# Row maxima turned by one matmul and subtracted by four row groups, projections in one run, and a new order on all engines

## The chip, the cores and the metric

The kernel runs on one core of one Trainium2 chip. The metric is the device time of one execution in microseconds, the median of several. A core has TensorE (matrix products, PE in the rows; PEld is its loading of the stationary operand), VectorE (DVE), ScalarE (ACT), GpSimd (POOL) and SyncE (SP), each with its own in-order queue, tied together by semaphores. Matrix products are written to PSUM, here one tensor `ps` of eight banks of 512 fp32 columns.

## The reference

One transformer block with modulated layer norms, for 8 batches of 256 tokens of width 128. Attention has 16 heads of 8 and a band mask; the feed-forward part is a mixture of 8 experts of width 64, of which two are chosen per token.

```python
h = _layernorm(x) * (1 + ca) + sa
# attention: B=8, S=256, 16 heads of 8
scores = einsum('bhqd,bhkd->bhqk', Q, K) / sqrt(8)
scores = where(abs(q - k) <= 32, scores, -inf)
out = einsum('bhqk,bhkd->bhqd', softmax(scores), V)
x = x + ga * (out @ W_o.T)
h = _layernorm(x) * (1 + cb) + sb
# experts: 2 groups of 4, then 2 experts of 8, by sigmoid(h @ gate_weight.T) + bias
y = sum_e combine_w[:, e] * ((silu(h @ gate[e].T) * (h @ up[e].T)) @ down[e].T)
x = x + gb * y
```

## The kernel before

One pass of the program handles the eight batches as a software pipeline. While batch i has its attention scores, batch i+1 has its first norm and projections, batch i-1 the end of attention, batches i-2 and i-3 the experts. For each engine the order is written out by hand: `first_step`, `second_step`, `third_step`, then `step(i)` for i = 3, 4, 5, then `seventh_step`, `last_step` and `drain`. Each is a list of calls such as `scores(i, 0)`; each call waits on its semaphores and issues its instructions. Nothing else sets the order, so what stands behind a waiting call on its engine waits too.

Attention of a batch. Queries and keys lie in blocks of 32; a tile `t` (0 or 1) is four query blocks. The 16 heads are four groups (`hg`) of four heads (`g`). `scores(i, t)` (lines 763 and 770) multiplies each key block, spread out by head in `k_bd`, with its two or three neighbouring query blocks of `q_sb`, and adds the mask. Each `hg` uses 32 rows of the array and writes its own PSUM bank 0 to 3: the partitions are (head, key), the columns three cells of 4 x 32 queries. `block_max` (1160) transposes blocks of 32 x 32 and takes each block's maximum, `row_maximum` (1169) the maximum over the three cells; its result lies by (head, query) on the partitions, with 16 numbers for `hg` and query block. The maximum must come off the scores along the columns. For that `shift_rows` (1177), once for each pair of `hg`, writes diagonal blocks of minus the maximum, and `subtract_max` (778) adds them to the scores by a product with a matrix of ones within each head, `quad_ones`: four products of 128 x 128 by 384 columns a tile. `exponentials` (533, ScalarE) makes `probs`, `weigh_values` (797) multiplies them with the values, again by pair: (t, pair) are four parts, which add up in bank OB = 4. `keep_o` (540) copies them to `o_t`; `transpose_o` (876), `normalise_o` (1280, 1284), `transpose_on` (883), `keep_on` (525), `output_projection` (890) and `residual` (1292) give `x1`.

Projections. `project_k` (735), `project_q` (740) and `project_v` (745) stand apart in the order and write banks W2 = 7, W0 = 5 and OB. `keep_k` (1152), `keep_q` (483), `keep_v` (491) copy them. The values go to HBM and back to be laid out by head (`place_values`, SyncE).

Experts. `transpose_x1` (718), `modulate_h2`, `logits` (808, the router), `route_compare`, `route_beats` and `route_weights` (small VectorE instructions), `up` (839 to 841, three fp32r products for each half), `tanh_gate` (546), `gate` (1255) and `gated` (1262), `weigh_experts` (359, GpSimd), `transpose_act` (856), `keep_act_t` (557), `down` (863), `gate_output` (1303), `add_output` (377). They use banks 5, 6 and 7. `keep_clock` (921) issues products whose result is not used, at places where TensorE would pause.

## Time and profile before

| | us |
|---|---|
| median of the timed runs | 164.77 |
| lowest and highest of three | 163.94, 164.79 |
| the profiled execution | 163.83 |
| its span, first to last instruction | 162.0 |
| TensorE busy | 151.1 |
| VectorE busy | 127.1 |
| ScalarE busy | 90.2 |
| GpSimd busy | 55.9 |

The granted clock of TensorE is 1.000 of full speed over the span. Busy time counts overlapping records of an engine once. Records of consecutive matmuls overlap, since their ends are modelled; what a block of matmuls takes from the queue is read from its start to the start of the next. An fp32 product in the program stands as two records; fp32r and bf16 products and fp32 transposes as one.

### The profile page before, as it was taken

The numbers are of one execution on the slowest core, as the hardware profiler recorded it, in microseconds if no ns is written. First come the engines' busy times: TensorE is split into PE (matmuls) and PEld (weight loads), VectorE is DVE, ScalarE is ACT, GpSimd is POOL, SyncE is SP. The second block draws the span as 40 slices with busy tenths as digits, with TensorE's granted clock in tenths as the row PEclk, the third lists the DMA queues.
The fourth block names the chain that finished last, engine by engine and source line by source line (L and its number), as shares of the span: only waits on it lengthen the run. The fifth ranks groups of instructions, "written<-read, shape, count | busy, mean of one in ns | idle before, by whom it ended". The sixth has DMA issues, their size and how long they took to land.

```text
span 162.0 us, 5111 instructions
## 1 busy us (share of the span) xinstructions
PE 151.1 (93%) x1976; PEld 123.2 (76%) x1976; DVE 127.1 (78%) x353; ACT 90.2 (56%) x172; POOL 55.9 (34%) x109
## 2 busy tenths in 40 slices
PE   6799989999899999999999999999999999888993
PEld 2376778787677898978887888789888986674773
DVE  3439496495988999897999789877988898587872
ACT  3234387556666656575747764785166428624740
POOL 6420072021540606521662147212251306426340
PEclk9999999999999999999999999999999999999999
DMA  4874134034103503510351013401250000010002
GB/s 134 239 210 28 8 38 32 4 65 28 10 0 46 59 0 67 37 34 4 65 33 35 0 35 43 32 0 35 34 36 0 9 28 0 6 32 0 0 4 65
DMA packets 47431, 6.23 MB, mean 38 GB/s; under 512 B 42416, under 2 KB 47024, under 8 KB 47408
## 3 DMA queue, kind: packets, MB, share of 16 engines
q1 hardware_dynamic: 47264, 5.90, 23.4%
q8 instruction: 16, 0.26, 0.7%
q14 instruction: 7, 0.06, 0.1%
q10 hardware_dynamic: 144, 0.00, 0.0%
HBM read 3.81 MB, written 2.10 MB: 36 GB/s over the span
## 4 chain that ended last, share of the span: by engine, by line
PE 71%; issue 9%; ACT 8%; DVE 6%; POOL 4%; POOLq 0%; ACTq 0%; DVEq 0%
PE ps L763 11%; PE ps L797 11%; PE ps L863 10%; PE ps L778 5%; PE ps L856 5%; PE ps L921 3%; PE ps L839 3%; ACT probs L533 3%; PE ps L841 3%; PE ps L840 3%; PE ps L718 3%; PE ps L808 2%; PE ps L740 2%; PE ps L745 2%; PE ps L890 2%
## 5 line engine op out<-in xcount | busy, mean ns | idle before, releaser
L1160 DVE TRANSPOSE_TENSOR_REDUCE blkmax<-ps 128x44 f32<-128x1408 f32 x16 | 26.4, 1648 | 11.7 <-PE ps L770 9.5
L797 PEld LDWEIGHTS ps<-probs,v_bd 128*36 128x36 f32 x640 | 21.5, 113 | 7.4 <-issue 4.7
L533 ACT ACTIVATE probs<-ps 128x704 f32<-128x704 f32 x32 | 23.0, 755 | 6.1 <-PE ps L778 5.6
L797 PE MATMUL ps<-probs,v_bd 128*36 128x96 f32 (+2 forms) x640 | 25.1, 228 | 0.8 <-ACT probs L533 0.5
L359 POOL TENSOR_TENSOR act_w<-act,cw 128x512 f32<-128x512 f32 x15 | 15.7, 1044 | 21.7 <-issue 13.7
L763 PEld LDWEIGHTS ps<-q_sb,k_bd 32*128 32x128 f32 x640 | 19.3, 186 | 4.3 <-issue 2.4
L763 PE MATMUL ps<-q_sb,k_bd 32*128 32x96 f32 (+2 forms) x640 | 21.3, 274 | 0.7 <-ACT probs L533 0.5
L778 PE MATMUL ps<-shift,quad_ones 128*128 128x384 f32 x64 | 16.9, 370 | 0.0
L863 PE MATMUL ps<-wd_sb,act_t 128*128 128x128 f32 x128 | 16.2, 280 | 0.6
L863 PEld LDWEIGHTS ps<-wd_sb,act_t 128*128 128x128 f32 x128 | 15.0, 191 | 2.0 <-ACT act_t L557 1.8
L546 ACT ACTIVATE tanh_g<-ps 128x512 f32<-128x512 f32 x14 | 8.3, 596 | 14.4 <-PE ps L841 14.4
L839 PE MATMUL ps<-w_hi,h_hi 128*128 128x512 f32 x32 | 13.4, 419 | 0.7 <-POOL h_lo L371 0.7
L334 POOL TENSOR_SCALAR veps<-mv 128x2 f32<-128x2 f32 x16 | 4.7, 294 | 26.9 <-DVE mv L1135 26.4
L371 POOL TENSOR_TENSOR h_lo<-h_t,h_hi 128x256 fp32r<-128x256 f32 x8 | 5.9, 732 | 22.0 <-ACT h_hi L505 21.9
L1177 DVE TENSOR_TENSOR shift<-row_max,con 128x256 fp32r<-128x256 f32 x32 | 12.8, 432 | 0.5
L841 PE MATMUL ps<-w_hi,h_lo 128*128 128x512 f32 x32 | 12.6, 393 | 0.0
L840 PE MATMUL ps<-w_lo,h_hi 128*128 128x512 f32 x32 | 12.5, 392 | 0.0
L557 ACT ACTIVATE act_t<-ps 128x512 f32<-128x512 f32 x16 | 9.4, 596 | 5.2 <-PE ps L856 5.0
L339 POOL TENSOR_TENSOR rstd<-veps,minus_half 128x2 f32<-128x2 f32 x16 | 11.4, 711 | 1.3
L778 PEld LDWEIGHTS ps<-shift,quad_ones 128*128 128x128 f32 x64 | 10.3, 190 | 1.0 <-DVE shift L1177 0.5
L921 PE MATMUL ps<-idle_bf 128*128 128x512 bf16 x28 | 9.5, 457 | 1.4 <-DVE idle_bf L1500 1.4
L1255 DVE SCALAR_TENSOR_TENSOR gate_a<-tanh_g,ps 128x512 f32<-128x512 f32 x14 | 9.6, 682 | 1.7 <-ACT tanh_g L546 1.4
(108 smaller groups left out, 283.5 us busy)
## 6 DMA issues: line engine op xcount, KB each, us to landing
x_sb<-x SPq DMA_DIRECT2D x8, 128.0 KB, 3.2
v_spill<-v_sb SPq DMA_DIRECT2D x8, 128.0 KB, 2.3
v_bd<-v_spill SPq DMA_DIRECT2D x32, 32.0 KB, 3.1
out<-out_sb SPq DMA_DIRECT2D x7, 128.0 KB, 2.0
wgu_sb<-w_gu SPq DMA_DIRECT2D x1, 512.0 KB, 4.3
wm_sb<-wmod SPq DMA_DIRECT2D x1, 256.0 KB, 3.8
wd_sb<-w_down SPq DMA_DIRECT2D x1, 256.0 KB, 5.2
con<-consts SPq DMA_DIRECT2D x1, 244.0 KB, 3.2
```

The source lines that it names most:

```text
L359: nc.gpsimd.tensor_tensor(act_w[:, t, :].rearrange("p (e i) -> p e i", e=E), act[:, t, :].rearrange("p (e i) -> p e i", e=E), view(cw[:, t ...
L533: nc.scalar.activation(probs[:, t, hgs, cols], ps[:, hgs, cols], ACT.Exp, scale=float(DH) ** -0.5).then_inc(probs_ready, 1)
L763: nc.tensor.matmul(view(ps[:, hg, at:at + 1], [[(QBT - 1) * KB, hi - lo + 1], [1, KB]]), k_bd[rows, kb].rearrange("p g k -> p (g k)"), vie ...
L778: last = nc.tensor.matmul(ps[:, hg, 0:CELLS * KB], quad_ones[:], view(shift[:, hg, 0:1], [[0, 3], [1, QBT * KB]]), start=False, stop=True, ...
L797: last = nc.tensor.matmul(ps[p0:p0 + VW, OB, c0 + lo * KB:c0 + (hi + 1) * KB], v_bd[:, i % VB, kb, hg, :], view(probs[:, t, hg, at:at + 1] ...
L839: nc.tensor.matmul(ps[:, bank, :], h2_hi[:, tok], w_hi[:, w], start=True, stop=False)
L840: nc.tensor.matmul(ps[:, bank, :], h2_hi[:, tok], w_lo[:, w], start=False, stop=False)
L841: last = nc.tensor.matmul(ps[:, bank, :], h2_lo[:, tok], w_hi[:, w], start=False, stop=True)
L863: last = nc.tensor.matmul(ps[:, down_bank(b, t), t * D:(t + 1) * D], act_t[:, t, c, :], wd_sb[:, c, :], start=(c == 0), stop=(c == NC_ - 1))
L921: nc.tensor.matmul(ps[:, bank, :], idle_bf[:, 0:128], idle_bf[:], start=True, stop=True)
L1160: nc.vector.tensor_reduce(blkmax[:, t, :, live(t):live(t) + LIVE], view(ps[:, 0, live(t) * KB:live(t) * KB + 1], [[BANK, NHG], [KB, LIVE], ...
L1177: nc.vector.tensor_tensor(shift[:, pair * PAIR:(pair + 1) * PAIR].rearrange("p h (q k) -> p (h q) k", k=KB), view(row_max[:, pair * PAIR, ...
```

## The change

1. The subtraction of the maxima. `spread_max` (VectorE) writes each of the 16 maxima into the column of its own head, zeros elsewhere, 64 numbers a partition. `turn_max` (TensorE) makes `max_by_head` the stationary operand and the matrix `C_REP` the moving one, 32 columns, into the unused columns 384 to 415 of bank 0. The maxima then lie on partitions by (hg, head, query block), with the 32 queries along the columns. `shift_rows`, now once a tile, multiplies them with -1 in the column of their block. `subtract_max` multiplies with `head_ones`, for each `hg` from its own 32 rows.
2. Queries, keys and values are projected in one call. `k_bd` and `q_sb` have two buffers. Queries and values both go to bank OB.
3. `x_sb` has eight buffers, and SyncE issues all loads of x by the start.
4. On TensorE waits that protect PSUM banks stand in the order instead of in the functions; `keep_act_t` and `keep_on` wait for the last readers of what they overwrite.
5. The written order is new on TensorE, VectorE, ScalarE and GpSimd, from the first step to the drain.

On TensorE, in the middle of a regular step. Before (`h_t` by line 808 is the router's input; 735 and 740 are keys and queries, 797 values times probabilities, `act_w` the weighted experts):
```order
L808 MATMUL ps<-gw_sb,h_t 128x8 x2
L778 MATMUL ps<-shift,quad_ones 128x384 x4
L735 MATMUL ps<-h_t,wqkv_sb 128x256
L797 MATMUL ps<-probs,v_bd 36x32 x2
L797 MATMUL ps<-probs,v_bd 36x64 x2
L797 MATMUL ps<-probs,v_bd 36x96 x4
L797 MATMUL ps<-probs,v_bd 36x64 x2
L740 MATMUL ps<-h_t,wqkv_sb 128x256
L797 MATMUL ps<-probs,v_bd 36x32 x2
L797 MATMUL ps<-probs,v_bd 36x64 x2
L797 MATMUL ps<-probs,v_bd 36x96 x4
L797 MATMUL ps<-probs,v_bd 36x64 x2
```
After, the first half of a regular step, from the router (778) on: 743 is the turn, 751 the subtraction, 809 the down projection, 706 and 819 transposes of x and o_t, 729 the scores:
```order
L778 MATMUL ps<-gw_sb,h_t 128x8 x2
L743 MATMUL ps<-con,max_by_head 128x32
L809 MATMUL ps<-wd_sb,act_t 128x128 x4
L751 MATMUL ps<-shift,head_ones 128x384 x4
L809 MATMUL ps<-wd_sb,act_t 128x128 x4
L706 MATMUL ps<-con,xn 128x128 x2
L819 MATMUL ps<-con,o_t 128x100 x4
L729 MATMUL ps<-q_sb,k_bd 128x32 x4
L729 MATMUL ps<-q_sb,k_bd 128x2x32 x4
L729 MATMUL ps<-q_sb,k_bd 128x3x32 x8
```
The subtraction, before followed by the key projection, stands between the halves of the down projection; the turn stands one half of the down projection ahead of it.

On VectorE, second tile of a regular step. Before:
```order
L1160 TENSOR_REDUCE blkmax<-ps 128x4x11
L1169 TENSOR_REDUCE row_max<-blkmax 128x16
L1177 TENSOR_TENSOR shift<-row_max,con 128x256 x2
L1255 SCALAR_TENSOR_TENSOR gate_a<-tanh_g,ps 128x512
L1262 TENSOR_TENSOR act<-gate_a,ps 128x512
L1152 TENSOR_TENSOR k_bd<-ps,con 128x1024
```
After (1147 block maximum, 1139 keys, 1156 row maximum, 1166 spread, 1252 and 1259 the first token half's gate, 1175 the shift):
```order
L1147 TENSOR_REDUCE blkmax<-ps 128x4x11
L1139 TENSOR_TENSOR k_bd<-ps,con 128x1024
L1156 TENSOR_REDUCE row_max<-blkmax 128x16
L1166 TENSOR_TENSOR max_by_head<-row_max,con 128x4x16
L1252 SCALAR_TENSOR_TENSOR gate_a<-tanh_g,ps 128x512
L1175 TENSOR_TENSOR shift<-ps,con 128x128
L1259 TENSOR_TENSOR act<-gate_a,ps 128x512
```
The copy of the keys moved in front of the row maximum, and the first gate stands between the spread and the shift.

The diff, cut to its core:

```diff
-C_NI = C_MASK + 2 * KB
-C_ONES = C_NI + KB
+C_ONES = C_MASK + 2 * KB
...
+C_QB = C_HEAD + G
+C_END = C_QB + QBT
...
-    c[:, C_NI:C_NI + KB] = np.where(r[:, None] == q[None], -1.0, 0.0)
-    c[:, C_ONES:C_ONES + 128] = g[:, None] == g[None]
+    c[:, C_ONES:C_ONES + 128] = (r // QBT)[:, None] == g[None]
...
+    c[:, C_QB:C_QB + QBT] = np.where((r % QBT)[:, None] == np.arange(QBT)[None], -1.0, 0.0)
...
-        q_sb = sb("q_sb", [128, S])
-        k_bd = sb("k_bd", [128, NKB, G, KB])
+        q_sb = sb("q_sb", [128, 2, S])
+        k_bd = sb("k_bd", [128, 2, NKB, G, KB])
...
-        shift = sb("shift", [128, NHG, QBT * KB], F32R)
+        max_by_head = sb("max_by_head", [128, NHG, KB])
+        shift = sb("shift", [128, QBT, KB], F32R)
...
             place_values(0)
+            load_x(4)
             place_values(1)
-            load_x(4)
+            load_x(5)
             place_values(2)
+            load_x(6)
+            load_x(7)
...
-            def project_k(b):
...
+            def project_qkv(b):
                 wait(pe, h_ready, b, 1, 1)
                 nc.tensor.matmul(ps[:, W2, 0:S], wqkv_sb[:, 1], h_t[:], start=True, stop=True).then_inc(k_ps, 1)
+                nc.tensor.matmul(ps[:, OB, 0:S], wqkv_sb[:, 0], h_t[:], start=True, stop=True)
...
+            def turn_max(i, t):
+                wait(pe, spread_ready, i, QT, t + 1)
+                nc.tensor.matmul(ps[:, 0, CELLS * KB:(CELLS + 1) * KB], max_by_head[:].rearrange("p h m -> p (h m)"),
+                                 con[:, C_REP:C_REP + KB], start=False, stop=True, skip_group_check=True)\
+                  .then_inc(turned_ps, 1)
+
             def subtract_max(i, t, pair):
-                wait(pe, shift_ready, i, PARTS, t * NPAIR + pair + 1)
+                wait(pe, shift_ready, i, QT, t + 1)
                 for hg in range(pair * PAIR, (pair + 1) * PAIR):
-                    last = nc.tensor.matmul(ps[:, hg, 0:CELLS * KB], quad_ones[:],
-                                            view(shift[:, hg, 0:1], [[0, 3], [1, QBT * KB]]),
+                    rows = slice(hg * KB, (hg + 1) * KB)
+                    last = nc.tensor.matmul(ps[:, hg, 0:CELLS * KB], head_ones[rows],
+                                            view(shift[rows, 0, 0:1], [[0, 3], [1, QBT * KB]]),
                                             start=False, stop=True, skip_group_check=True)
                 last.then_inc(shifted_ps, 1)
...
-            def shift_rows(i, t, pair):
+            def spread_max(i, t):
                 wait(dve, rowmax_ready, i, QT, t + 1)
+                wait(dve, turned_ps, i, QT, t)
...
+                nc.vector.tensor_tensor(
+                    view(max_by_head[:, 0, 0:1], [[KB, NHG], [QBT, G], [1, QBT]]),
+                    view(row_max[:, 0, 0:1], [[QBT, NHG], [0, G], [1, QBT]]),
+                    view(con[:, C_DEN:C_DEN + 1], [[0, NHG], [1, G], [0, QBT]]), ALU.mult).then_inc(spread_ready, 1)
+
+            def shift_rows(i, t):
+
+                wait(dve, turned_ps, i, QT, t + 1)
                 wait(dve, shifted_ps, i, PARTS, t * NPAIR)
                 nc.vector.tensor_tensor(
-                    shift[:, pair * PAIR:(pair + 1) * PAIR].rearrange("p h (q k) -> p (h q) k", k=KB),
-                    view(row_max[:, pair * PAIR, 0:1], [[1, PAIR * QBT], [0, KB]]),
-                    view(con[:, C_NI:C_NI + 1], [[0, PAIR * QBT], [1, KB]]), ALU.mult).then_inc(shift_ready, 1)
+                    shift[:], view(ps[:, 0, CELLS * KB:CELLS * KB + 1], [[0, QBT], [1, KB]]),
+                    view(con[:, C_QB:C_QB + 1], [[1, QBT], [0, KB]]), ALU.mult).then_inc(shift_ready, 1)
...
             def step(i):
+                wait(pe, probs_ready, i - 1, PARTS, 4)
                 scores(i, 0)
...
+                turn_max(i, 0)
+                wait(pe, actt_ready, i - 3, NT, 2)
+                down(i - 3, 0)
+                subtract_max(i, 0, 0)
+                subtract_max(i, 0, 1)
```

## Rows read from the trace of the kernel before

**Rows 1.** The page's busy line: busy us, share of the span, instructions.
```profile
PE 151.1 (93%) x1976; PEld 123.2 (76%) x1976; DVE 127.1 (78%) x353; ACT 90.2 (56%) x172; POOL 55.9 (34%) x109
```

**Rows 2.** Stretches: length, busy us of each engine, PEclk, DMA share, GB/s.
```profile
37.07:55.26 18.19, 16.93 (x248) 13.50 (x244) 15.18 (x40) 11.57 (x25) 6.74 (x14) 1.00 0.32 28
72.10:88.90 16.80, 16.61 (x239) 14.19 (x238) 14.69 (x42) 10.81 (x22) 6.78 (x13) 1.00 0.25 33
120.53:139.79 19.26, 18.31 (x266) 15.06 (x262) 14.77 (x40) 11.46 (x24) 6.08 (x10) 1.00 0.04 9
139.79:162.00 22.21, 18.20 (x112) 13.96 (x112) 16.08 (x52) 8.22 (x15) 7.74 (x12) 1.00 0.07 20
```

**Rows 3.** TensorE's timeline in one step: start us, length us, instructions.
```profile
81.12 0.29 PE L770 MATMUL ps<-mask_bf,rep_bf 32*128 32x256 bf16 x4
81.34 1.44 PE L797 MATMUL ps<-probs,v_bd 128*36 128x64 f32 x40
82.71 0.44 PE L718 MATMUL ps<-con,xn 128*128 128x128 f32 x2
...
84.38 0.51 PE L808 MATMUL ps<-gw_sb,h_t 128*128 128x8 f32 x4
84.74 0.95 PE L778 MATMUL ps<-shift,quad_ones 128*128 128x384 f32 x4
85.53 0.59 PE L735 MATMUL ps<-h_t,wqkv_sb 128*128 128x256 f32 x2
86.19 0.82 PE L797 MATMUL ps<-probs,v_bd 128*36 128x32 f32 x20
86.94 0.70 PE L740 MATMUL ps<-h_t,wqkv_sb 128*128 128x256 f32 x2
87.57 0.82 PE L797 MATMUL ps<-probs,v_bd 128*36 128x32 f32 x20
...
93.71 0.61 PE L745 MATMUL ps<-wqkv_sb,h_t 128*128 128x128 f32 x4
94.08 0.59 PE L778 MATMUL ps<-shift,quad_ones 128*128 128x384 f32 x2
94.51 0.60 PE L890 MATMUL ps<-wo_g,on_t 128*128 128x128 f32 x4
94.87 0.60 PE L778 MATMUL ps<-shift,quad_ones 128*128 128x384 f32 x2
95.31 0.39 PE L839 MATMUL ps<-w_hi,h_hi 128*128 128x512 f32 x1
```

**Rows 4.** TensorE's timeline, first projections of batch 0.
```profile
8.09 0.67 PE L735 MATMUL ps<-h_t,wqkv_sb 128*128 128x256 f32 x2 [0.63 <-ACT h_t L475]
...
9.48 0.59 PE L921 MATMUL ps<-idle_bf 128*128 128x512 bf16 x2
```

**Rows 5.** VectorE's timeline in the same step.
```profile
79.50 0.35 DVE L1205 TENSOR_REDUCE rank<-ebeat 128x16 f32<-128x224 f32 x1
...
80.82 0.68 DVE L1255 SCALAR_TENSOR_TENSOR gate_a<-tanh_g,ps 128x512 f32<-128x512 f32 x1
...
82.14 1.64 DVE L1160 TRANSPOSE_TENSOR_REDUCE blkmax<-ps 128x44 f32<-128x1408 f32 x1
83.81 0.21 DVE L1169 TENSOR_REDUCE row_max<-blkmax 128x16 f32<-128x48 f32 x1
84.06 0.76 DVE L1177 TENSOR_TENSOR shift<-row_max,con 128x256 fp32r<-128x256 f32 x2
...
86.54 1.22 DVE L1152 TENSOR_TENSOR k_bd<-ps,con 128x1024 f32<-128x1024 f32 x1
```

**Rows 6.** Groups by form, VectorE: busy us, mean ns; idle before.
```profile
L1311 DVE TENSOR_TENSOR y_last<-ps,gate_row 128x128 f32<-128x128 f32 x2 | 0.6, 292 | 2.0 <-PE ps L863 2.0
```

**Rows 7.** Groups by form, ScalarE: copies of o_t, tanh.
```profile
L540 ACT ACTIVATE o_t<-ps 36x512 f32<-36x512 f32 x16 | 9.4, 589 | 0.4
...
L546 ACT ACTIVATE tanh_g<-ps 128x512 f32<-128x512 f32 x14 | 8.3, 596 | 14.4 <-PE ps L841 14.4
```

More of the change, by code:

```diff
@@ L319, in _ @@
             step(B - 2)
-            for b in range(B - 4, B - 1):
+            for b in range(B - 1 - 3, B - 1):
                 sp.wait_ge(out_ready, b + 1)
@@ L1056, in drain @@
                 output_projection(B - 1)
+                wait(pe, yg_ready, B - 3, 1, 1)
                 up(B - 2, 0)
@@ L1279, in normalise_o @@
                 wait(dve, ot_ps, i, 1, 1)
+                wait(dve, ont_ps, i, 1, 0)
                 nc.vector.reciprocal(
```

597 lines of the change are left out of this document (287 added, 310 removed).

## The prediction, made before the result was known

> **What bounds the kernel now.** I read the busy line first: TensorE is busy 93% of the span, VectorE 78%, ScalarE 56%, GpSimd 34% [rows 1]. Shares are averages, so I then read the stretches [rows 2]. Their bounds are the starts of the key-by-query products of a batch (call them S; S0 and S1 are its two tiles of query blocks). In the regular stage one batch passes every 16.80 us, and TensorE is busy 16.61 of it, VectorE 14.69, ScalarE 10.81, GpSimd 6.78. That is a TensorE bound with VectorE close behind. In 120.53 to 139.79 and from there to the end TensorE leaves 0.9 and 4.0 us idle: the drain is a chain through all engines.
>
> Third, I read one step of TensorE's own queue, start to start, because overlapping records hide what a block costs [rows 3]. The subtraction of the row maxima (line 778) stands there twice: four matmuls adjacent, 84.74 to 85.53, 0.79 us; and split in pairs, 94.08 to 94.51 and 94.87 to 95.31, 0.43 + 0.44. That is 1.66 us a batch. Keys, queries and values stand in three places: 85.53 to 86.19 (0.66, of which some 0.2 waits for the exponentials), 86.94 to 87.57 (0.63), 93.71 to 94.08 (0.37): 1.66. Another 0.2 is TensorE's idle time in the step's stretch, 16.80 - 16.61 [rows 2]. So a step holds 16.4 us of work and 0.4 of waits.
>
> **The subtraction.** The new one uses 32 rows of the array for each of the four head groups, where each used all 128. The nearest row of that form is the mask product: four matmuls on four row groups, 256 columns each, and the next block starts 0.22 us after the first of them [rows 3]. Its 256 columns and the 384 of the subtraction stand in the relation of 0.12 to 0.18 us by the present 0.79/4 for 384. That gives a lower bound of 0.22 + 0.07 = 0.29 us for four. The upper bound is the present 0.79, if they queue one behind another. I take 0.36, near the mask row, with 0.07 for the change from 128-row to 32-row form in front. The turn is one matmul in the program, two in the records, as all fp32 here. The router's product (line 808) is the nearest: four records in 0.36 us, 84.38 to 84.74, so 0.18 for two; the upper bound adds the same gap of some 0.12 that the mask product leaves behind it, 0.30. I take 0.22. A tile then costs 0.58, two tiles 1.16 against 1.66: 0.50 us less per batch. The ends are 2 x (0.29 + 0.18) = 0.94 (0.72 less) and 2 x (0.79 + 0.30) = 2.18 (0.52 more).
>
> The skill has a rule in each direction. The Trainium skill (TensorE: Matmul & The Clock Gate, Part 3) says that four K=32 matmuls on separate row groups start a few ns apart and measured 3.07 times the throughput; by it a tile's subtraction would be 0.79/3.07 = 0.26 us, and the kernel's sum would fall by some 1.6 us more. The Trainium skill (TensorEngine Tiling (Array Packing), Key Properties) also says that a change of the tiling mode drains the engine, which speaks against breaking one 128-row queue by short 32-row pieces; the trace bears this out in kind, since the mask product is left only 0.22 us after its start; what it could take is the rival below in which nothing is gained.
>
> **Projection and value products.** In one run the three projections took 8.09 to 9.48, 1.39 us [rows 4]. With an entry of 0.1 that is 1.49 against 1.66, and most of the difference is the wait. The value products (line 797) pay for it: now two of the four parts are one run, 81.34 to 82.71 (1.37), and the others cost 0.75 each, 2.87 in all; apart, four times 0.75 plus entries, 3.1. That is 0.23 more. The transposes of the activations become one run of eight, with one such gap less, some 0.15. Together these edits are worth 0.1 less; bounds -0.3 and +0.4, from the same rows, by whether an entry costs nothing or 0.15 each. TensorE's work for a step: 16.4 - 0.5 - 0.1 = 15.8, which I round up to 15.9 for the one more change of form.
>
> **VectorE.** Each batch loses four shift instructions of 0.76/2 = 0.38 us [rows 5], 1.5 us, and gains two spreads and two shifts. The spread writes 64 numbers a partition from the 16 of row_max; the nearest row is the row maximum, 0.21 [rows 5], the bound above is today's shift, 0.38. I take 0.24 with the gap. The new shift makes 128 per row and reads PSUM as line 1311 does, 0.29 [rows 6], so 0.33 with the gap. 2 x 0.57 = 1.14, about 0.35 less a batch. VectorE's load falls to 14.3 us plus its gaps; it does not bind by its sum.
>
> It can bind by its order. From block maximum to subtraction the queue now goes VectorE, TensorE, VectorE. Today 0.96 us pass from the end of the block maximum (82.14 + 1.64) to the subtraction at 84.74 [rows 3, 5]. The new round is 0.24 (row maximum) + 0.24 (spread) + 0.05 + 0.37 (a turn until its result, from the router's row: 0.51 less two spacings) + 0.05 + 0.33 = 1.3 us, 0.3 longer. Behind a turn that waits stand, in TensorE's in-order queue, a down projection in the first half of a step, and a value product, the output projection and the subtraction in the second. Laid out from S0 at 0, with the blocks above: S0 1.4, value product 2.1, transposes 3.3, router 3.7; block maximum 1.6 to 3.25, spread done 3.75, so the turn at 3.8 waits 0.1. The down projection waits for ScalarE's second act_t copy, 4.4, 0.3 us. Shifts are ready at 4.9 (a layer norm of 0.8 stands in between, beside the turn), the subtraction runs at 5.4. ScalarE has two copies of o_t (0.59 each, [rows 7]) in front of its exponentials, which end at 7.2; TensorE reaches S1 at 7.4. Block maximum of S1 8.9 to 10.6, keep_k (1.22, [rows 5]), row maximum and spread to 12.3; the turn is reached at 12.3, the second subtraction at 13.7, the last up product at 14.1 to 15.5, the value product to 16.2. Then S0 again. Waits of some 0.4 us stay: 15.9 + 0.4 = 16.3 us a step, 0.5 less.
>
> **The three stages.** Regular part, from S0 of batch 3 (55.26) to S0 of batch 7 (120.53): four steps, 4 x 0.5 = 2.0 us. Start, to 55.26: the chain products, maxima, exponentials, products sets it through the first two batches (the turn's 0.3 more a tile is met by 0.43 less for the subtraction that ends it), S0 of batch 2 comes at 36.8 for 37.07 [rows 2]; seven more clock-keeping matmuls stand in waits. In batch 2 the queue is full and gains as a step does: 0.8 us in all. The x loads of batches 4 to 7, now issued between and behind the first value transfers, cost nothing on SyncE's queue, since x is read a batch later; if they delayed the values of batch 1, 0.3. Last step, 120.53 to 139.79: a step's 0.5 and what the earlier start of its S0 leaves (one value product less before it), but its subtraction is split in pairs and so is paid three times: 0.7. The drain, 22.2 us, keeps its code and its chain: 0. Sum 2.0 + 0.8 + 0.7 = 3.5. The profiled execution took 163.83 (span 162.0 and 1.8 around it), so 160.3 by it; it is 0.9 below the median of the runs, 164.77, against which the forecast is 161.3.
>
> **Rivals.**
> - *The full gain.* The 0.4 us of waits a step fall away too, or the subtraction costs 0.29. A step is 15.9: 4 x 0.9, 1.0 and 1.1 at the ends, 5.7 in all, 159.1. For it: every wait in my layout is under 0.3. Against: ScalarE's copies are where they are.
> - *Nothing is gained.* The changes of form (one more run of value products, two subtractions, each way) cost 0.15 more than I price, and waits for act_t and act take the rest; the step stays at 16.7 and the start gains nothing: 164.4. For it: VectorE and TensorE hand to each other twice more a batch.
> - *Slower by VectorE's loop.* The last up product now stands at the end of a step. After it come the end of its last matmul and tanh (0.2 + 0.6, [rows 7]), gate and product (80.82 to 82.14, 1.32, [rows 5]), then the block maximum and spread of the next batch, 1.64 + 0.5, before TensorE may turn: 4.3 us. TensorE has 4.4 us of work for that time (value product, S0, value product, transposes, router). If the routing weights (1.32 us of small instructions ahead of that gate, 79.50 to 80.82) end later than the tanh by more than 0.1 us, all of that excess is added each step. With 0.9 of it a step is 17.1: 4 x 0.3, 0.3 in the last, 0.6 at the start, 2.1 more, 166.9. My layout has the weights end 0.2 after the tanh, so it decides soon. Against: what makes them late is a late output projection, which would itself come later in a slower step.
> - *The row groups do not run at once* for this type. Then subtraction and turn cost up to 0.52 more a batch, some 0.4 a step of the forecast's work too much: 166.5. Against: the mask row.
>
> **Numbers.** Half a per cent, 0.8 us, is about what a measurement can tell from no change. Forecast 0.50 (its own range 159.8 to 163.0), full gain 0.17, nothing 0.16, VectorE's loop 0.12, no concurrency 0.05. Faster by over 0.8 us: 0.50 + 0.17 = 0.67, and 0.01 of the case without gain, 0.68; within 0.16; slower 0.16. The range that should hold eight in ten runs from 158.6 to 165.2: it takes in the full gain, the case without gain and the near end of the losses.
>
> **What would show it.** In the changed profile the four subtractions of a tile should start within 0.05 us of each other and the block after them follow in 0.3 to 0.4; the turn's records should take under 0.25; S0 to S0 should be 16.0 to 16.6 in batches 3 to 6; the end of VectorE's product of the second act tile should lie just before the block maximum; the drain from the transpose of o_t of batch 7 should be unchanged at about 20 us of queue. A step of 16.8 or more, a turn preceded by more than 0.3 of idle TensorE, or a subtraction over 0.6 would show it wrong, and in that order I would look for the cause.

## The result and the profile after

The changed kernel takes 165.15 us (median of 20 runs, 164.68 to 166.34) against 164.7 for the kernel before beside it: ratio 1.0067, 95% interval 1.004 to 1.0093. It is slower by little, where 161.3 and faster was forecast. The profiled execution has a span of 162.5 us at a granted clock of 0.999. First the busy line of its page, which answers to [rows 1]:

```profile
PE 152.3 (94%) x2010; PEld 122.4 (75%) x2015; DVE 122.0 (75%) x354; ACT 88.5 (54%) x172; POOL 54.5 (34%) x109
```

VectorE lost 5 us of work, as meant, and TensorE gained 1. Two stretches that answer to [rows 2]: a regular step; and from S0 of batch 7 to the transpose of o_n of batch 7. The rest, from there to the end of the span, takes 19.12 us. Columns: stretch, length, then the busy time of each engine, granted clock, DMA share, GB/s.

```profile
70.29:87.23 16.94, 16.93 (x246) 14.25 (x242) 14.19 (x42) 10.38 (x22) 6.57 (x14) 1.00 0.23 26
120.36:143.38 23.02, 21.79 (x308) 17.93 (x307) 19.32 (x60) 13.17 (x26) 9.36 (x15) 1.00 0.08 10
```

A step is 16.94 us for 16.80 [rows 2], and TensorE is busy in 16.93 of it. So no wait shows as idle time, and what TensorE does takes longer. (A wait can hide in the busy time, since the ends of the records are modelled; the pair after_noturn and noturn_early below shows how much.) Its queue in that step, with the blocks that answer to [rows 3] (start, modelled length, operands, array rows and columns):

```profile
72.67 1.04 PE L802 MATMUL ps<-con,act_w 128*128 128x128 f32 x8
73.55 0.56 PE L778 MATMUL ps<-gw_sb,h_t 128*128 128x8 f32 x4
74.05 0.41 PE L743 MATMUL ps<-con,max_by_head 128*128 128x32 f32 x2
74.47 1.16 PE L809 MATMUL ps<-wd_sb,act_t 128*128 128x128 f32 x8
75.56 0.44 PE L751 MATMUL ps<-shift,head_ones 32*128 32x384 f32 x4
75.93 1.16 PE L809 MATMUL ps<-wd_sb,act_t 128*128 128x128 f32 x8
76.92 0.38 PE L706 MATMUL ps<-con,xn 128*128 128x128 f32 x2
...
78.97 0.70 PE L714 MATMUL ps<-h_t,wqkv_sb 128*128 128x256 f32 x2
...
80.30 0.47 PE L791 MATMUL ps<-w_hi,h_hi 128*128 128x512 f32 x1
```

```profile
82.88 0.31 PE L743 MATMUL ps<-con,max_by_head 128*128 128x32 f32 x2
83.12 0.81 PE L767 MATMUL ps<-probs,v_bd 128*36 128x64 f32 x20
83.86 0.71 PE L833 MATMUL ps<-wo_g,on_t 128*128 128x128 f32 x4
84.50 0.45 PE L751 MATMUL ps<-shift,head_ones 32*128 32x384 f32 x4
84.88 0.50 PE L791 MATMUL ps<-w_hi,h_hi 128*128 128x512 f32 x1
85.22 0.40 PE L792 MATMUL ps<-w_lo,h_hi 128*128 128x512 f32 x1
```

Read start to start. The subtraction (751) takes 0.37 and 0.38 us, the second turn (743) 0.24, the first 0.42 (a wait is in it, as after_early shows), the projections in one run 80.30 - 78.97 = 1.33. These are the prices of the forecast. But the blocks around them have grown: the down projection has halves of 1.09 and 0.99, 2.08 in all, where it takes 1.79 in the old order without its wait (before_early, below), and the output projection takes 0.64 for 0.36 [rows 3]. In VectorE's queue [rows 5] the spread and the shift are as small as forecast:

```profile
71.84 1.65 DVE L1147 TRANSPOSE_TENSOR_REDUCE blkmax<-ps 128x44 f32<-128x1408 f32 x1 [0.15 <-PE ps L736]
...
73.76 0.23 DVE L1166 TENSOR_TENSOR max_by_head<-row_max,con 128x64 f32<-128x64 f32 x1
...
74.58 0.26 DVE L1175 TENSOR_TENSOR shift<-ps,con 128x128 fp32r<-128x128 f32 x1
```

Two theories follow. *Changes of form*: the array works in three forms here, 128 rows by 128 columns, 32 rows (scores, mask, new subtraction) and 36 columns (value products); each time the form changes the block before ends later and the block behind starts slower, and this eats what the row groups save. From S0 to S0 the order before changes the form 9 times, the new one 14 times. *Order and waits*: the new order brings waits, and the blocks' growth is these.

### The profile page after: what moved, and what is told of

Read it like the earlier page. It is cut to its first block, busy times and chain, and to the rows that moved or that the text cites. A ratio compares the mean times of both kernels' runs of the same rounds, so it can differ in the third digit from the quotient of the medians.

```text
span 162.5 us, 5181 instructions
## 1 busy us (share of the span) xinstructions
PE 152.3 (94%) x2010; PEld 122.4 (75%) x2015; DVE 122.0 (75%) x354; ACT 88.5 (54%) x172; POOL 54.5 (34%) x109
## 4 chain that ended last, share of the span: by engine, by line
PE 73%; DVE 10%; issue 5%; DMA 3%; SPq 3%; ACT 3%; POOL 2%; POOLq 0%; ACTq 0%
PE ps L767 13%; PE ps L729 11%; PE ps L809 8%; PE ps L802 5%; PE ps L791 4%; PE ps L792 3%; PE ps L793 3%; DMA x_sb<-x 3%; PE ps L751 3%; PE ps L743 3%; PE ps L851 3%; PE ps L706 2%; PE ps L714 2%; PE ps L833 2%; PE ps L819 2%
## 5 line engine op out<-in xcount | busy, mean ns | idle before, releaser
L767 PE MATMUL ps<-probs,v_bd 128*36 128x64 f32 (+2 forms) x640 | 26.2, 228 | 0.3
L326 POOL TENSOR_SCALAR veps<-mv 128x2 f32<-128x2 f32 x16 | 3.6, 224 | 48.1 <-DVE mv L1122 47.7
L809 PE MATMUL ps<-wd_sb,act_t 128*128 128x128 f32 x128 | 17.7, 284 | 0.2
L331 POOL TENSOR_TENSOR rstd<-veps,minus_half 128x2 f32<-128x2 f32 x16 | 12.3, 767 | 9.3 <-ACT xn L450 8.0
L791 PE MATMUL ps<-w_hi,h_hi 128*128 128x512 f32 x32 | 14.0, 438 | 0.9 <-DVE y_g L1301 0.5
L859 PE MATMUL ps<-idle_bf 128*128 128x512 bf16 x30 | 10.1, 446 | 1.8 <-DVE idle_bf L1498 1.4
L1139 DVE TENSOR_TENSOR k_bd<-ps,con 128x1024 f32<-128x1024 f32 x8 | 9.7, 1208 | 1.9 <-PE ps L714 1.9
L527 ACT ACTIVATE o_t<-ps 36x512 f32<-36x512 f32 x16 | 9.5, 591 | 1.9 <-PE ps L767 1.5
L545 ACT ACTIVATE act_t<-ps 128x512 f32<-128x512 f32 x16 | 8.9, 596 | 2.5 <-PE ps L802 2.5
L465 ACT ACTIVATE h_t<-ps,mod 128x256 f32<-128x256 f32 x8 | 6.5, 814 | 6.3 <-PE ps L706 6.3
```

What stands on the lines that cost most here:

```text
L331: nc.gpsimd.tensor_tensor(rs[:], veps[:], minus_half[:], ALU.pow).then_inc(rs_done, 1)
L767: last = nc.tensor.matmul(ps[p0:p0 + VW, OB, c0 + lo * KB:c0 + (hi + 1) * KB], v_bd[:, i % VB, kb, hg, :], view(probs[:, t, hg, at:at + 1] ...
L791: nc.tensor.matmul(ps[:, bank, :], h2_hi[:, tok], w_hi[:, w], start=True, stop=False)
L809: last = nc.tensor.matmul(ps[:, down_bank(b, t), t * D:(t + 1) * D], act_t[:, t, c, :], wd_sb[:, c, :], start=(c == 0), stop=(c == NC_ - 1))
L859: nc.tensor.matmul(ps[:, bank, :], idle_bf[:, 0:128], idle_bf[:], start=True, stop=True)
L1139: nc.vector.tensor_tensor(k_bd[:, b % 2], view(ps[:, W2, 0:1], [[1, NKB], [0, G], [NKB, KB]]), view(con[:, C_HEAD:C_HEAD + 1], [[0, NKB], ...
```

## The experiments

Ratios are to the kernel before on the same chip, with 95% intervals.

**probe.** One look at the kernel before with the new subtraction in the old order, and behind its end a tail of products that wait for no other engine: 128-row fp32 blocks of eight records in turn with the new subtraction, with the old one, and with 36-column products, and each of these once in a run of its own kind.

```diff
+                for _ in range(6):
+                    full(4, 6)
+                    rows32(1)
+                full(4, 6)
+                rows32(6)
```

> A probe behind the last output of a kernel of the order before (it carries the new subtraction; only its tail is read, and that tail is extra work whose results are not used). It issues blocks of a plain fp32 product on 128 rows (F), of the subtraction on four times 32 rows (R), of the old subtraction on 128 rows, and of the value product with 36 columns (W), each once as one run and once in turn with F. Theory 'changes of form': every change between F and R or F and W costs TensorE 0.1 to 0.2 us beyond the blocks themselves, so F, R, F, R takes about 0.3 us more per pair than the same blocks sorted, and F with the old subtraction under 0.1 more. Rival 'waits': a change of form costs nothing by itself (under 0.03 us a pair), and what the changed kernel lost are waits for other engines.

```profile
168.44 6.42 PE L934 MATMUL ps<-con 128*128 128x128 f32 x56
174.78 0.45 PE L941 MATMUL ps<-shift,head_ones 32*128 32x384 f32 x4
175.16 1.16 PE L934 MATMUL ps<-con 128*128 128x128 f32 x8
176.25 0.45 PE L941 MATMUL ps<-shift,head_ones 32*128 32x384 f32 x4
...
183.57 1.32 PE L941 MATMUL ps<-shift,head_ones 32*128 32x384 f32 x24
184.83 1.16 PE L934 MATMUL ps<-con 128*128 128x128 f32 x8
...
188.12 1.05 PE L934 MATMUL ps<-con 128*128 128x128 f32 x8
188.93 0.95 PE L947 MATMUL ps<-shift,head_ones 128*128 128x384 f32 x4
...
195.33 4.49 PE L947 MATMUL ps<-shift,head_ones 128*128 128x384 f32 x24
```

In a run of its own kind the new subtraction takes 1.26/6 = 0.21 us for four. In turn with 128-row blocks it takes 0.38, and the block behind 1.09, where eight such records take (174.78 - 168.44) x 8/56 = 0.91 in a run. So the pair costs 1.47 for 0.21 + 0.91 = 1.12: 0.35 for two changes of form, as the first theory had it. The old subtraction, of the form of its neighbours, takes 0.79 in turn and the block behind it 0.81, 1.60 in all, and costs nothing extra (0.72 + 0.91 in runs). So the new subtraction saves 0.13 a pair, from a block whose own time fell by 0.41. The 36-column products show the same: 0.79 and 1.08 in turn (202.51 to 203.30 and 201.43 to 202.51), 1.87 for at most 0.69 + 0.91, so 0.27 for two changes.

**before_newsub.** The old order with the new subtraction and the turn. The first turn stands two blocks ahead of its subtraction, the second one block, so that the turn's round through VectorE has some cover; the two pairs of the first subtraction, apart before, stand side by side.

```diff
                 down(i - 3, 1)
+                turn_max(i, 0)
                 transpose_on(i - 1)
                 project_v(i + 1)
                 subtract_max(i, 0, 0)
-                output_projection(i - 1)
                 subtract_max(i, 0, 1)
+                output_projection(i - 1)
```

> The order before, with only the subtraction changed: spread, turn, one shift a tile, subtraction on four row groups, its two pairs adjacent. Theory 'changes of form': a step of 16.80 us loses 1.66 and gains 2 x 0.38 (subtraction) + 2 x 0.24 (turn) + 0.4 (first and last matmul of the blocks beside four more changes), 16.8; time within 0.5% of before, ratio 1.00. Rival 'the order is what lost': the subtraction is worth the 0.5 us a batch that I forecast, so 4 us less, ratio 0.976.

169.96 us, ratio 1.036 (1.032 to 1.040): slower than either theory. Its step is 17.43 us with TensorE busy 16.98, so 0.45 of it shows as waiting:

```profile
74.84:92.27 17.43, 16.98 (x243) 13.65 (x243) 14.02 (x42) 10.82 (x22) 6.67 (x13) 1.00 0.25 32
...
87.91 0.29 DVE L1209 TENSOR_TENSOR shift<-ps,con 128x128 fp32r<-128x128 f32 x1 [0.50 <-PE ps L779]
```

The second shift waits 0.50 us for the turn, and the up product in front of that turn takes 0.52 us (86.95 to 87.47) for 0.23 without a wait. So in this order the round from VectorE to TensorE and back costs time. TensorE is busy 0.37 longer than before (16.61), but part of this is such hidden waiting, so the run doesn't say how much work the new subtraction adds. It does not show a gain in work, which speaks for the first theory.

**after_oldsub.** The new order with the old subtraction: both shifts and the 128-row products, no turn.

```diff
-                turn_max(i, 0)
...
-                    rows = slice(hg * KB, (hg + 1) * KB)
-                    last = nc.tensor.matmul(ps[:, hg, 0:CELLS * KB], head_ones[rows],
+                    last = nc.tensor.matmul(ps[:, hg, 0:CELLS * KB], head_ones[:],
```

> The changed kernel with the old subtraction (two shifts a tile, 128 rows, no spread and no turn), all else as changed. Theory 'changes of form': the step of 16.94 us loses the turn with its waits (0.66), the 0.75 of the subtraction and 0.38 beside it, and gains 1.58: 16.7; in all 1.6 us less than the changed kernel, ratio to before 0.997. Rival 'the order is what lost, the subtraction gains': 4 us more than the changed kernel, ratio 1.03.

165.66 us, ratio 1.0088 (1.0058 to 1.0118), neither theory. In the new order the two ways of subtracting come out almost alike in the whole time. One wait appears that the turn had stood in:

```profile
70.05:87.10 17.05, 16.69 (x243) 14.58 (x239) 14.83 (x42) 10.39 (x22) 6.57 (x14) 1.00 0.18 23
...
73.30 0.56 PE L770 MATMUL ps<-gw_sb,h_t 128*128 128x8 f32 x4
74.22 1.16 PE L801 MATMUL ps<-wd_sb,act_t 128*128 128x128 f32 x8 [0.36 <-ACT act_t L544]
```

**after_fullrows.** The new kernel, turn and order kept, but the subtraction on all 128 rows.

```diff
-                    rows = slice(hg * KB, (hg + 1) * KB)
-                    last = nc.tensor.matmul(ps[:, hg, 0:CELLS * KB], head_ones[rows],
-                                            view(shift[rows, 0, 0:1], [[0, 3], [1, QBT * KB]]),
+                    last = nc.tensor.matmul(ps[:, hg, 0:CELLS * KB], head_ones[:, hg],
+                                            view(shift[:, 0, 0:1], [[0, 3], [1, QBT * KB]]),
```

> The changed kernel with one edit: the four subtractions of a tile use all 128 rows of the array again (the stationary operand is zero outside the head group's rows), the turn and the order stay. Theory (the saving of the row groups is mostly eaten by two changes of form per tile): the subtraction's own block grows from 0.37 to 0.79 us, its neighbours shrink by some 0.3 per tile, so a regular step goes from 16.94 to about 17.2 and the whole from 165.15 to about 167, ratio to before 1.014. Rival (the changes of form cost nothing here, neighbours stay): 0.42 us more per tile, 17.8 a step, about 171.5 in all, ratio 1.04.

167.63 us, ratio 1.0237 (1.0202 to 1.0273), a step of 17.17: near the first theory, far from the second's 171.5. The same blocks as above, with nothing else changed:

```profile
76.95 1.16 PE L808 MATMUL ps<-wd_sb,act_t 128*128 128x128 f32 x8
77.87 0.95 PE L750 MATMUL ps<-shift,head_ones 128*128 128x384 f32 x4
78.66 1.05 PE L808 MATMUL ps<-wd_sb,act_t 128*128 128x128 f32 x8
79.55 0.38 PE L706 MATMUL ps<-con,xn 128*128 128x128 f32 x2
...
86.47 0.71 PE L832 MATMUL ps<-wo_g,on_t 128*128 128x128 f32 x4
86.94 0.94 PE L750 MATMUL ps<-shift,head_ones 128*128 128x384 f32 x4
87.72 0.39 PE L790 MATMUL ps<-w_hi,h_hi 128*128 128x512 f32 x1
87.95 0.40 PE L791 MATMUL ps<-w_lo,h_hi 128*128 128x512 f32 x1
```

This is the price list. The row groups take the subtraction from 0.79 + 0.78 to 0.37 + 0.38, 0.82 less a step. Before and behind them the halves of the down projection go from 0.92 and 0.89 to 1.09 and 0.99, the output projection from 0.47 to 0.64, the first product of the up projection from 0.23 to 0.34: 0.27 + 0.17 + 0.11 = 0.55 given back. That leaves 0.27; the whole step gains 0.23 (17.17 for 16.94).

**before_p32** and **before_p128.** The kernel before with one small foreign piece in the middle of each up product of batches 0 to 5, on 32 rows or on all 128. They ask for the price of a change of form in the kernel as it is.

```diff
+            def piece(bank):
+                for n in range(4):
+                    rows = slice(0, KB)
+                    nc.tensor.matmul(ps[:, bank, 0:KB], rep_bf[rows], mask_bf[rows, 0],
+                                     start=True, stop=True)
```

> The kernel before with four bf16 matmuls of 32 columns on 32 rows of the array put between the two halves of the up product, for batches 0 to 5, both tiles: 12 places, two of them in each regular step, written where the next matmul starts afresh, and read by nobody. Theory (leaving and entering the 128-row form costs some 0.38 us, by the tail measurement): the halves lie 0.38 plus the own time of about 0.1 further apart, 2 x 0.48 = 1.0 us more a step and about 4.8 in all where TensorE binds, 169.5, ratio 1.03. Rival (only own time): 2 x 0.1 a step, 1.2 in all, ratio 1.007.

> The control of the run with the 32-row pieces: the same four bf16 matmuls of 32 columns at the same 12 places, now on all 128 rows of the array, so that no form changes. Theory (what the 32-row pieces cost, 0.39 us between the halves of the up product, is nearly all change of form): here the halves lie 0.05 to 0.12 further apart, a step is 16.80 + 0.1 to 0.25, and the whole 164.5 to 166, ratio 1.002 to 1.012, against 1.030 with the 32-row pieces. Rival (four more weight loads and starts cost it, whatever the form): again 0.39 each, 17.6 a step, ratio 1.03.

168.86 us, ratio 1.0296 (1.0266 to 1.0327), and 165.79, ratio 1.012 (1.0072 to 1.0167). First the 32-row pieces, then the 128-row ones:

```profile
81.05 0.39 PE L849 MATMUL ps<-w_hi,h_lo 128*128 128x512 f32 x1
81.38 0.26 PE L815 MATMUL ps<-mask_bf,rep_bf 32*128 32x32 bf16 x4
...
81.90 0.39 PE L848 MATMUL ps<-w_lo,h_hi 128*128 128x512 f32 x1
```

```profile
79.14 0.40 PE L849 MATMUL ps<-w_hi,h_lo 128*128 128x512 f32 x1
79.38 0.27 PE L815 MATMUL ps<-mask_bf,rep_bf 128*128 128x32 bf16 x4
...
79.81 0.39 PE L848 MATMUL ps<-w_lo,h_hi 128*128 128x512 f32 x1
```

From the product before the piece to the second one behind it, 0.46 without a piece, it takes 0.85 with 32 rows and 0.67 with 128. So a piece costs 0.39 or 0.21, and 0.18 of it is the change of form: 0.09 because the last 128-row product is left later (0.33 for 0.24), the rest in the piece and behind it. The first theory had nearly all of 0.39 for the form; half is the broken run itself, which costs without any change of form.

**after_noturn.** The new kernel without the turn. It leaves out a part of the computation: the shift is made from the maxima as they lie, so what is subtracted are not the maxima of the queries. The run only prices the turn.

```diff
-                turn_max(i, 0)
...
-                    shift[:], view(ps[:, 0, CELLS * KB:CELLS * KB + 1], [[0, QBT], [1, KB]]),
+                    shift[:], view(max_by_head[:, 0, 0:1], [[0, QBT], [1, KB]]),
```

> The changed kernel without the turn: the shift is made from the spread maxima directly, so the maxima subtracted are not those of the queries (this part of the computation is changed). It prices the turn with its wait on VectorE. Theory (the turn costs its two 0.24 us blocks and some 0.15 of wait per step, and nothing takes their place): 16.94 - 0.6 = 16.35 a step, about 160.7 in all, ratio to before 0.976. Rival (another wait, for ScalarE's copies or exponentials, takes most of it): a step of 16.8, 164.2 in all, ratio 0.997.

164.23 us, ratio 0.9997 (0.9968 to 1.0027), a step of 16.79: the rival. With this wait in place the turn costs only 0.15 us a step, because the wait for ScalarE's second act_t copy comes back where the first turn stood (0.36 of idle time before 73.32).

**after_join, after_wv, after_last, after_both.** Attempts to win back changes of form in the new order: the value products of the second tile adjacent (after_join), those of the first tile adjacent (after_wv), blocks of one form put together from S0 of batch 7 on (after_last), and after_wv with after_last. The core of the second, then of the third:

```diff
                 wait(pe, k_ready, i + 1, 1, 1)
                 transpose_on(i - 1)
-                turn_max(i, 1)
+                weigh_values(i, 0, 0)
                 weigh_values(i, 0, 1)
+                turn_max(i, 1)
```

```diff
                 transpose_act(B - 3, 0)
-                weigh_values(B - 1, 1, 0)
                 transpose_act(B - 3, 1)
+                weigh_values(B - 1, 1, 0)
                 weigh_values(B - 1, 1, 1)
```

> The changed kernel with one edit to TensorE's order: the third part of the value products (t=1, pair 0) moves behind the scores of the next batch, next to the fourth, so that a step has 12 changes of form for 13. Theory 'changes of form': 0.15 to 0.2 us less a step, 1 us less in all, ratio to before 1.000. Rival 'waits': the value products' place does not matter, TensorE's queue keeps its length, ratio stays 1.007.

> The changed kernel with the turn of the second tile and the transpose of o_n moved out from between the two value products of the first tile, in the three regular steps (order: transpose of o_n, both value products, turn, output projection, subtraction): 2 changes of form less per step. Theory (a pair of changes costs 0.3 us here): a step of 16.65 for 16.94, and 0.9 us less in all, 164.3, ratio to before 0.998 to 1.002. Rival (forms cost nothing, the order does): 16.94 or more, since the turn now comes 0.7 us later and the subtraction may wait for the shift: 17.0, ratio 1.008.

> The changed kernel with only its last step and drain merged: the two value products of batch 6 adjacent, both pairs of the first subtraction adjacent, the last two value products adjacent; six changes of form and one split of a subtraction less, all behind S0 of batch 7. Theory: from that S0 to the transpose of o_n of batch 7 it takes 22.1 for 23.02, and 164.3 in all, ratio 1.001. Rival (that stretch is set by waits for VectorE and ScalarE, not by the forms: it was 23.0 to 23.1 in three variants with 13 and with 19 changes): 22.9 or more, no gain, ratio 1.007.

> Both edits of the two runs before it in one kernel. If both theories hold, their gains add up: a step of 16.65, the last stretch 22.1, about 163.5 in all, ratio 0.993, slightly below before. If only the first holds 164.3, ratio 0.999; if none, 165.2 or more.

They take, in this order, 166.5 us (ratio 1.0121, 1.0076 to 1.0165), 166.47 (1.0134, 1.0096 to 1.0171), 166.07 (1.0125, 1.0073 to 1.0176) and 167.03 (1.0152, 1.0102 to 1.0203). None is faster. after_join (13 changes of form a step for 14, by the count above; its expectation counts one less each) has a step of 16.82, 0.12 less, near what its theory had, but the whole is not shorter. Its profile, of an execution of 168.26 us, shows where the gain goes. Ahead of S0 of batch 3 the value product is missing as cover, and TensorE idles 0.74 us for the exponentials (54.84). In the 4.3 us behind this pause the granted clock is 0.60 in the mean, so mostly at its lower level (1.2 of 2.4 GHz), and the scores take 1.85 us for 1.14 and the value products 2.08 for 1.38. That is 1.6 us in this execution, the slowest of the six; the others have no profile, and that the pause made the clock fall is not shown. And from S0 of batch 7 to the transpose of o_n it takes 23.33 for 23.02.

In after_wv the joined value products take 1.36 for 1.49, 0.13 less. But the last up product in front of the transpose of o_n takes 0.44 for 0.33, since the transpose waits for the copy of the keys; the transpose, now next to value products, 0.37 for 0.27; and the subtraction 0.52 for 0.38, since the up product behind it waits for VectorE's act. A step is 17.14.

In after_last the stretch from S0 of batch 7 to the transpose of o_n takes 23.71 us for 23.02, with fewer changes of form, because it waits longer for the other engines, here 0.84 for 0.47, and 0.52 for GpSimd's act_w at 139.02:

```profile
129.79 0.50 PE L791 MATMUL ps<-w_hi,h_hi 128*128 128x512 f32 x1 [0.84 <-DVE y_g L1301]
```

There the second theory holds: the last stretch takes 23.0 to 23.2 us with the new order, with the old subtraction, on full rows and without the turn alike.

**before_join** and **before_split.** The same question in the old order: value products of the second tile joined by projecting the queries earlier, and those of the first tile split by two transposes.

```diff
                 project_k(i + 1)
-                weigh_values(i, 1, 0)
                 project_q(i + 1)
+                weigh_values(i, 1, 0)
                 weigh_values(i, 1, 1)
```

> The kernel before with one edit in the regular step: the query projection stands directly behind the key projection, so that the value products of the second tile are one run of 40 (one 128-row run between two 36-column runs less, three steps have it). Theory (two changes of form less cost about 0.3 us): a step of 16.5 for 16.80 in batches 3 to 5, 0.9 less in all, 163.8, ratio 0.994. Rival (a change of form costs nothing, only blocks move): 16.8 a step, ratio 1.000. At this size the profile's steps tell more than the total.

> The kernel before with the transpose of the second norm (two 128-row matmuls) moved in between the two value products of the first tile, in the three regular steps: two changes of form more a step, nothing else. Theory (joining such a pair in the changed kernel gave 0.13): a step of 16.93 to 17.0 for 16.80, 0.4 to 0.6 more in all, ratio 1.003. Rival (breaking a run costs as little as 0.02): 16.80. The steps of the profile tell, not the total.

165.95 us, ratio 1.0117 (1.0079 to 1.0154), and 166.13, ratio 1.0105 (1.0043 to 1.0167). Steps are 17.22 and 17.38; neither theory has these. The join saves work (TensorE busy 16.46 for 16.61) but the query projection waits 0.64 for VectorE's act. The split costs 0.58 a step. About 0.28 of it is a wait for ScalarE's norm (the value product in front of the transpose takes 1.03 for 0.75, 0.22 of this as idle time), so about 0.30 is the broken run with its two changes of form, more than either theory had.

**before_early, after_early, noturn_early.** The wait for the second act_t copy taken out of three kernels: the down projection of the first tile starts with the first copy, and writes the bank that this copy has emptied. In the old kernel this is two lines.

```diff
-            return {B - 2: OB, B - 1: 2 + t}.get(b, W1)
+            return {B - 2: OB, B - 1: 2 + t}.get(b, W0)
...
-                wait(pe, actt_ready, b, NT, NT if b < B - 2 else t + 1)
+                wait(pe, actt_ready, b, NT, t + 1)
```

> The kernel before, with the down projection of a batch's first tile released by ScalarE's first act_t copy and not by the second; for this its output goes to the bank of the first tile's transposes, which is free by then. Theory (0.28 us a step of TensorE's time before the down projection is this wait, and nothing is late next): a step of 16.5 for 16.80, with the last step 1.2 to 1.5 us less in all, 162.6, ratio 0.992. Rival (the second copy is then waited for between the tiles, or the bank makes the next up product wait): no gain, ratio 1.000.

> The changed kernel with the same edit. Here the turn stands in front of the down projection and fills part of that wait (0.42 from the turn's start to the down projection, against 0.24 for the second turn). Theory: the step falls by 0.18, from 16.94 to 16.76, and the whole to 164.2, ratio to before 1.000. Rival (the wait moves to the shift of the first subtraction, which is then reached 0.18 sooner): 16.94, ratio 1.007.

> The changed kernel without the turn (the shift is made from the spread maxima directly, so the maxima subtracted are not those of the queries) and with the same edit. Theory (the turn cost only 0.15 a step since it stood in the wait for the copies): without that wait the step is 16.79 - 0.36 = 16.43, so that against the run with the turn and this edit the turn costs 0.33 to 0.48 a step, and the whole is 161.9, ratio 0.986. Rival (another wait, for the first copy or the shift, takes its place): 16.7 or more, ratio 0.997.

163.36 us, ratio 0.9922 (0.9888 to 0.9956); 164.35, ratio 1.0009 (0.9979 to 1.004); 162.24, ratio 0.9841 (0.9783 to 0.99). The first two are as the theory had them. noturn_early, which leaves out the same part of the computation as after_noturn, gains more than its theory: a step of 16.30 for 16.43. The steps, in this order:

```profile
72.78:89.20 16.42, 16.36 (x239) 14.17 (x238) 14.59 (x42) 10.81 (x22) 6.79 (x13) 1.00 0.25 34
```

```profile
70.60:87.32 16.72, 16.72 (x246) 14.17 (x242) 14.18 (x42) 10.39 (x22) 6.56 (x14) 1.00 0.23 26
```

```profile
69.93:86.23 16.30, 16.30 (x243) 13.65 (x239) 14.06 (x42) 10.26 (x22) 6.56 (x14) 1.00 0.20 24
```

In before_early's queue the down projection takes 76.98 - 75.19 = 1.79, with no idle time in front:

```profile
75.19 1.95 PE L863 MATMUL ps<-wd_sb,act_t 128*128 128x128 f32 x16
76.98 0.38 PE L883 MATMUL ps<-con,o_n 128*128 128x128 f32 x2
```

Without this wait a step is 16.42 in the old kernel, 16.72 in the new one, 16.30 in the new one without the turn. before_early changes two lines of the old kernel and beats both.

noturn_early also shows how a wait hides in busy time. Its router block is followed by the down projection 0.43 us after its start:

```profile
73.18 0.56 PE L772 MATMUL ps<-gw_sb,h_t 128*128 128x8 f32 x4
73.61 1.16 PE L803 MATMUL ps<-wd_sb,act_t 128*128 128x128 f32 x8
```

In after_noturn and after_oldsub the same block has the same length, 0.56, and the next one starts after 0.92. The wait is 0.92 - 0.43 = 0.49, and this is what the step loses without it, 16.79 - 16.30; as idle time only 0.36 is shown. In the new kernel the first turn filled this gap, so there the edit gains 16.94 - 16.72 = 0.22, from a step that was busy throughout. And after_oldsub without the wait would have a step of 17.05 - 0.49 = 16.56 by this estimate.

## Why the prediction was wrong, step by step

**TensorE's work in the new step is the step that failed.** The forecast had 16.4 us of work before and 15.9 after. Measured are 16.42 (before_early) and 16.72 (after_early). That is 0.8 us a step too little, against 0.4 of waits that the forecast added and of which the runs have some 0.2 (16.94 - 16.72). The sum by its own terms:

| term of a step | forecast | measured |
|---|---|---|
| four subtractions of a tile | 0.36, 0.07 of it for the form | 0.37, 0.38 |
| the turn, two a step | 0.44 | 0.42 (16.72 - 16.30) |
| what neighbours lose to the 32-row subtraction | 0 beyond that 0.07 | 0.55 (after_fullrows) |
| the three projections | 1.49 | 1.33 |
| value products | 3.1 | 2.99 |
| transposes of the activations in one run | 0.15 less | 0.19 less |

The row groups run at once, the turn costs what the router's rows said, and the joined runs bring more than priced. What was mis-sized is the change of form: I put 0.07 in front of a subtraction, read at the mask product. But the mask product stands behind the scores, which are 32-row products themselves. So its rows cannot show what it costs to leave a 128-row block. In the place where the subtraction stands, that is 0.17 on the block in front and 0.10 or 0.11 on the block behind.

With it the subtraction's gain is gone. Forecast: 1.16 against 1.66, 0.5 less. Measured: 0.75 + 0.42 + 0.55 = 1.72 against the 1.57 of the old subtraction in the same order, 0.15 more. Whole steps agree: 16.72 against some 16.56. Of this the four row groups give 0.26 (16.56 to 16.30) and the turn takes 0.42. So 0.66 of the missing 0.8 lies here.

**The order is the smaller part.** The forecast gave the edits of the order 0.1 less and 0.1 for form, nothing in sum. Measured from 16.42 to 16.56 it is 0.14 more. By blocks, start to start, before_early against after_oldsub: the three projections save 0.31 (1.33 for 1.64), the transposes of the activations 0.20, the subtraction with its pairs side by side 0.10. Blocks that border on others now have grown by 0.76: the transpose of o_n by 0.15, the value products 0.13, the up products 0.11, the output projection 0.10, the transpose of o_t 0.10, those of the norms 0.08, the router 0.07, the down projection 0.02. The two sums leave 0.15. That a change of form is the cause for each of these blocks is argued from their places and not tried one by one. What a pair of changes costs is no one number: 0.13 in after_wv, 0.18 in before_p32 less before_p128, some 0.30 with the broken run in before_split, 0.35 in the probe.

**Waits, and luck.** The 16.4 us of work before came out right by luck. The forecast took 0.19 of idle time and 0.2 in the key projection for the waits. But the wait for the act_t copy alone is 0.38 (16.80 - 16.42), half of it hidden in busy time. The key projection's 0.66 does hold a wait for the exponentials, and before_early has it still (0.65): the value product behind it starts at 86.19 [rows 3], 0.06 after the first of the two exponentials (0.75 each) ends, 85.38 + 0.75 = 86.13. In before_early it is the same 0.05.

```profile
85.38 1.41 ACT L533 ACTIVATE probs<-ps 128x704 f32<-128x704 f32 x2
```

```profile
115.52 0.59 PE L740 MATMUL ps<-h_t,wqkv_sb 128*128 128x256 f32 x2
116.04 0.81 PE L797 MATMUL ps<-probs,v_bd 128*36 128x64 f32 x20
```

Where such a projection stands between a 128-row block and value products in the kernel before and nothing is late, it takes 0.52. So some 0.14 of the 0.66 is a wait and 0.09 the change of form, and the work of the step before is nearer 16.3. The forecast also took this wait off twice, in the 16.4 and in the 0.17 that the projections were to save; by its own terms the edits of the order cost 0.1 instead of saving 0.1.

Slips without weight: 256 and 384 columns stand as 0.13 to 0.20 us by 0.79/4, not 0.12 to 0.18, with the same difference; 0.51 less two spacings of the router is 0.33, not 0.37; and the fourth of the "regular" steps, 105.70 to 120.53, takes 14.83 us before, not 16.80.

**The start and the last step.** S0 of batch 7 starts at 120.36, for 120.53 before, but one value product (0.75) more is still to do; so the first seven batches lost some 0.6 where 2.8 was forecast as gain. From there to the transpose of o_n of batch 7 it takes 23.02 for 21.77 (120.53 to 142.30 before): 0.75 is that value product, 0.5 waits and forms, where 0.7 was to be gained. Two waits, 0.47 for y_g and 0.32 for act, hold it. The rest of the drain is 19.1 for 19.7 us, 0.6 less, where no change was forecast. The traces show where: from the output projection of batch 7 to the transpose of its second norm it is 4.08 us for 4.81. Before, VectorE is still at the routing weights of batch 6 when this projection is done, and adds the residual 1.40 us after the projection's start (144.56); now these weights come earlier in its written order, and it is 0.75 (145.03). No run changes this alone.

**The rivals.** *Nothing is gained* is what happened, and by the mechanism it named, though larger: 164.4 forecast, 165.15 measured, changes of form first and a wait for act_t of 0.2 a step second. The Trainium skill (TensorEngine Tiling (Array Packing), Key Properties) says that a change of the tiling mode drains the engine. The trace agrees: 0.17 us on the down projection's half in front of the subtraction. The page's rule was in the text and got 0.16; the runs show that it deserved a price of its own in the sum. The 3.07 times of the Trainium skill (TensorE: Matmul & The Clock Gate, Part 3) holds in a run: 4.33/6 = 0.72 us for four in the old form (195.33 to 199.66 in the tail) against 0.21, 3.4 times. Between 128-row blocks it is 1.60 against 1.47 for the pair. *VectorE's loop* did not bind: VectorE waits 0.15 us for TensorE before the block maximum (71.84). The first turn does start 0.06 us behind the spread (73.76 + 0.23, 74.05), and the router block in front of it takes 0.50 for the 0.43 of noturn_early, so this round is just at its limit. *Row groups not at once* is refuted by 0.37. *The full gain* lacked 0.8 of work.

## What to carry to other kernels

Price a short block in another form of the array by what its neighbours lose as well as by its own rows, and read that price at a place where the same two forms meet; here, of 0.82 us of saved time, 0.55 went back to the neighbours, and the turn took more than the rest. A block of work that is removed or moved may have stood in a wait: take the wait out first (before_early, two lines, 0.8%), and then see what the block is worth. A step with TensorE busy in all of it can still hold a wait: after_early took 0.22 us out of a step that was busy 16.93 of 16.94. Read blocks start to start against a run in which nothing is late.

## What the runs showed of the hardware

- A 128-row block is left 0.09 us (fp32r products of 512 columns: 0.33 for 0.24) to 0.17 us (fp32 products, down projection: 1.09 for 0.92) later when a block in another form follows.
- A pair of changes of form around four 32-row products costs 0.35 us between 128-row fp32 blocks (probe: 1.47 for 1.12), and 0.27 around 36-column products (1.87 for 1.60).
- Breaking a run costs even in the same form: four bf16 products of 32 columns between fp32r products cost 0.21 us (0.67 for 0.46).
- Four 32-row products of 384 columns take 0.21 us in a run of their kind, and 0.37 to 0.38 when a 128-row block follows.
- Idle time shows a wait too small: 0.36 where the next block came 0.49 us later than without the wait (after_oldsub and after_noturn against noturn_early).
- In the one profile of after_join the granted clock was 0.60 in the mean over 4.3 us behind a pause of 0.74 us, and 1.00 before and after; forty score records took 1.85 us for 1.14.
